# Audio tower with mixture of experts: a drain behind each gather and scatter of GpSimd, and another order of a bias' split, slots and one-hots

## The chip, the cores and the metric

The kernel runs on one core of one Trainium2 chip. The metric is the device time of one launch in microseconds, as the median of several executions. The engines are TensorE (PE in the rows), VectorE (DVE), ScalarE (ACT), GpSimd (POOL) and SyncE (SP); each has its own instruction order, and semaphores tie them together.

## What is computed

Sixteen recordings of 64 channels and 750 samples are cut into patches of 200 samples, which gives 4096 tokens. Each passes a Fourier transform and a two-layer network into 128 features, then attention with sparsemax (8 heads, 256 tokens per sequence), then eight experts, each of which chooses its own 1024 tokens. The part that the change is about is the last one:

```python
x_flat = x.reshape(N, Dd)                      # N = 4096, Dd = 128
logits = x_flat @ Wr                           # 8 experts
probs = jax.nn.softmax(logits, axis=0)         # over the tokens
vals, idx = jax.lax.top_k(probs.T, C)          # C = 1024 for each expert
selected = x_flat[idx]
h = gelu(einsum('ecd,edf->ecf', selected, W1) + b1)      # F = 512
out_e = einsum('ecf,efd->ecd', h, W2) + b2
output = zeros_like(x_flat).at[idx.reshape(-1)].add(vals[..., None] * out_e)
```

The kernel computes in f32, with bf16 for masks and one-hots.

## The kernel before

**Up to the routing.** The spectrum and sixteen rounds of attention, one for each 512 tokens, follow a plan (`PLAN`, `STEPS`) that fixes the order of TensorE's, ScalarE's and VectorE's work. GpSimd only does small things there: `power()` (lines 505 to 508), the reciprocal square root of a layer norm, and `anymore()` (line 514). The normalised rows go to the DRAM tensor `rows2`.

**Routing.** VectorE takes the largest logit of each expert, GpSimd reduces it over the partitions (line 558), then ScalarE exponentiates, VectorE sums, and GpSimd reduces again (line 560). Fifteen steps of `two_bits` find each expert's threshold; `ranks` then numbers the chosen tokens. Before line 558 GpSimd splits the output bias of expert 7 into three bf16 parts (lines 538 to 556). The build puts a change of GpSimd's configuration (MODIFY_POOL_CONFIG) ahead of the first reduction, and another behind the second.

**Expert 7** is computed densely for all tokens (`every_hidden`, `every_out`), in between the other work. VectorE adds its rows to `h` with weights (`every_added`, line 1673, 32 instructions for all 4096 tokens); ScalarE tells through the semaphore `every_y_ok` that rows are there.

**Experts 0 to 6** pass a pipeline of six steps:

1. `one_hots(e)` on VectorE (lines 1606 to 1625) builds one-hot matrices from the ranks; line 1603 is one of their 32 comparisons, line 1615 the largest multiplication.
2. `expert_slots(e)` on TensorE (line 1106) multiplies them, and `slots(e)` on VectorE (lines 1631 to 1643) turns the product into 1024 row numbers.
3. `gather(e)` on GpSimd (lines 575 to 582): 8 indirect DMAs of 128 rows of 512 bytes from `rows2` into `xg`.
4. `expert_columns`, `expert_hidden`, `expert_out` on TensorE (lines 1115, 1130, 1144) with ScalarE's copies and gelus (line 631).
5. `weighted(e)` on VectorE (lines 1650 to 1669), in two halves: line 1662 adds the bias in PSUM, line 1664 multiplies by the weights into `y`. The semaphore `y_ok` counts the halves.
6. `scatter(e)` on GpSimd (lines 584 to 606): 8 indirect DMAs of 128 rows into the expert's own plane in DRAM, 4 for each half. Between the halves of experts 1 to 5 one DMA adds the plane of the expert before to `h` (line 600). A wait ahead of the fifth scatter (line 592) lets VectorE reuse `y`.

GpSimd's order is gathers 0 to 3, then scatter 0, gather 4, scatter 1, gather 5, scatter 2, gather 6, scatters 3 to 6. Line 587 is the wait for the first half of `y`, line 578 that for a gather's slots. Its sequencer runs ahead of its cores: requests wait in a queue. TensorE does expert e+1's columns between expert e's first and second layer, and slots for expert e+3 behind these columns. VectorE's order is one-hots, slots, and `weighted` of three experts before.

Behind the last scatter a no-op (line 617) raises `issued`; VectorE then adds plane 5 (line 1708), SyncE loads plane 6 in quarters, VectorE adds them (line 1714) and SyncE stores the result.

Of the kernel before, what the change touches and what calls it, by code (L numbers as in the profile page):

```python
# [130 lines left out]
def audio_tower(nc, x, tok_w1, tok_b1, tok_w2, tok_b2, w_qkv, w_out, b_out, w_r, e_w1, e_b1, e_w2, e_b2,  # L131
# [25 lines left out]
    E = w_r.shape[1]  # L157
# [13 lines left out]
    with ctx:  # L171
# [311 lines left out]
        def _(g):  # L483
# [53 lines left out]
            attention_round(BEFORE)  # L537
            power()
            g.wait_ge(sems["every_w_in"], 64)
# [15 lines left out]
            g.drain()  # L555
            g.engine_nop().then_inc(sems["b2_ok"], 1)
            g.wait_ge(sems["mx_in"], 1)
            g.partition_all_reduce(all_max[:, :], lg_max[:, :], P, RMAX).then_inc(sems["mx_ok"], 1)
# [16 lines left out]
            def gather(e, p, half=range(CT)):  # L575
                g.wait_ge(sems["slots_ok"], e + 1)
                g.wait_ge(sems["xg_used"], e + 1)
                g.sem_inc(sems["pool_held"], 1)
                for s in half:
                    g.indirect_dma_start(xg[p][:, s, :], None, rows2[:, :],  # L580
                                         bass.IndirectOffsetOnAxis(ap=gather_at[p][:, s:s + 1], axis=0))\
                        .then_inc(sems[f"xg_in{p}"], 16)

            def scatter(e):
# [3 lines left out]
                for s in range(CT):  # L588
                    if s == CT // 2:
# [3 lines left out]
                        if 0 < e < GE - 1:  # L593
# [3 lines left out]
                            else:  # L597
# [7 lines left out]
                    g.indirect_dma_start(plane[e][:, :], bass.IndirectOffsetOnAxis(ap=add_at[p][:, s:s + 1], axis=0),  # L605
                                         y[p][:, s, :], None).then_inc(sems[f"y_out{p}"], 16)

            g.sem_inc(sems["y_free"], 2)
# [11 lines left out]
        def _(a):  # L620
# [167 lines left out]
            every_gelu(4, 1, c.job(1))  # L788
            every_out(3)
            every_gelu(5, 0, c.job(3))  # L790
            every_gelu(5, 1, c.job(1))
# [31 lines left out]
        def _(t_):  # L823
# [298 lines left out]

            def expert_hidden(n, p, ahead=None):
                t_.wait_ge(sems[f"ew_in{p}"], (n + 1) * 64)
                jobs = []
                for m in range(F // P):
# [5 lines left out]
                    done(jobs[-1], last)  # L1132
                    if m == 1 and ahead is not None:
                        expert_slots(ahead)
# [22 lines left out]
            columns_used(expert_columns(0, 0))  # L1157
            hidden = expert_hidden(0, 0, 2)
            columns = expert_columns(0, 1)
# [9 lines left out]
            for e in range(1, GE):  # L1169
                hidden = expert_hidden(e // 2, e % 2)  # L1170
                if e + 1 < GE:
                    columns = expert_columns((e + 1) // 2, (e + 1) % 2)
                    if e + 3 < GE:
                        expert_slots(e + 3)
                    columns_used(columns)
                expert_out(e % 2, hidden)

        @block.vector
        def _(v):
# [500 lines left out]
            one_hots(1, quarters=True)  # L1680
            slots(0, 1, first=True)
            one_hots(2)
            slots(1, 0)
            c.up("slot3", 1)
            one_hots(3)
            slots(1, 1)
            v.tensor_tensor(every_w[:, :], pr[:, E - 1, :], sel[:, E - 1, :], ALU.mult)
            v.wait_ge(sems["every_y_ok"], 1)
            v.drain()
            every_added(range(0, 6))  # L1690
            weighted(0, 0)
            v.wait_ge(sems["every_y_ok"], 2)
            v.sem_inc(sems["held"], 1)
            every_added(range(6, 8))
            v.drain().then_inc(sems["every_ok"], 1)
            for e in range(4, GE):
                one_hots(e)
                slots(e // 2, e % 2)
                weighted((e - 3) // 2, (e - 3) % 2)
            for e in range(GE - 3, GE):  # L1700
                weighted(e // 2, e % 2)
# [57 lines left out]
```

## Time and profile before

| | |
|---|---|
| median of 3 runs | 884.61 us (882.42 to 889.73) |
| the profiled execution, as a run | 887.41 us |
| its span, first to last instruction | 885.6 us |
| mean granted TensorE clock | 0.912 of full speed |
| PE busy | 720.7 us (81%) |
| DVE busy | 604.1 us (68%) |
| ACT busy | 473.0 us (53%) |
| POOL busy | 163.7 us (18%), 121 us of it behind 660 us |
| chain that ended last | PE 35%, DVE 32%, issue 13%, ACT 6%, an unknown queue 4% |

The chain of work that ended last is followed back from the last instruction, at each step to what released it; "issue" is time in which the engine waited for nothing that the profile shows, and "remote" or "another core or an unknown queue" is a wait whose releaser it does not find. Busy time leaves out waits, semaphores and the sequencers' work. A name with a q (POOLq) is an engine's sequencer. For a gather or scatter the row's duration is GpSimd's making of descriptors, not the transfer.

### The profile page before, as it was taken

How to read it: one execution, taken by the hardware profiler on the slowest of the kernel's cores; microseconds unless marked ns; L12 is line 12 of the kernel's file. 1: busy time of each engine (PE TensorE's matmuls, PEld its weight loads, DVE VectorE, ACT ScalarE, POOL GpSimd, SP SyncE). 2: the span in 40 equal slices, each digit the busy share in tenths (PEclk: the TensorE clock that was granted, in tenths of full speed). 3: DMA queues.
4: the chain of work that ended last, by engine and by line, in shares of the span. 5: the costliest groups of instructions: out<-in, count | busy, mean ns of one | idle time of the engine just before them, and what ended most of it. 6: DMA issues, size and time to landing. Idle time of an engine off the chain costs nothing.

```text
span 885.6 us, 13171 instructions
## 1 busy us (share of the span) xinstructions
PE 720.7 (81%) x4268; PEld 470.2 (53%) x4268; DVE 604.1 (68%) x2163; ACT 473.0 (53%) x697; POOL 163.7 (18%) x213
## 2 busy tenths in 40 slices
PE   5598769768999999999999987776977966855970
PEld 3244355456575575665755755544654645543750
DVE  1877787788979968979689688717886562440124
ACT  3857647447777777877787778533322320122220
POOL 1000000001001010010000100021006575555451
PEclk9889989979999999999999999777988998877995
DMA  7791000000000000000000000020001121675778
GB/s 249 278 333 48 1 1 1 0 1 14 1 2 14 1 2 13 1 14 1 1 13 2 13 1 14 25 65 1 1 2 43 36 70 42 152 155 118 160 165 291
DMA packets 29608, 51.99 MB, mean 59 GB/s; under 512 B 8299, under 2 KB 22976, under 8 KB 27658
## 3 DMA queue, kind: packets, MB, share of 16 engines
q1 hardware_dynamic: 24358, 33.03, 11.8%
q0 software_dynamic: 4944, 17.83, 8.8%
q8 instruction: 34, 0.56, 0.3%
q14 instruction: 60, 0.49, 0.2%
q10 hardware_dynamic: 212, 0.08, 0.0%
HBM read 40.97 MB, written 22.54 MB: 72 GB/s over the span
## 4 chain that ended last, share of the span: by engine, by line
PE 35%; DVE 32%; issue 13%; ACT 6%; DVEq 4%; another core or an unknown queue 4%; POOL 2%; DMA 2%; POOLq 1%; ACTq 1%; SPq 0%
PE ps L903 5%; DVE back L1285 4%; PE ps L1130 4%; PE ps L1144 4%; DVE top L1288 3%; PE ps L948 3%; DVE top L1256 3%; DVE back L1263 3%; PE ps L921 3%; PE ps L858 2%; PE ps L997 2%; PE ps L971 2%; DVE front L1603 2%; ACT front L631 2%
## 5 line engine op out<-in xcount | busy, mean ns | idle before, releaser
L631 ACT ACTIVATE front<-ps 128x1024 f32<-128x1024 f32 (+1 forms) x136 | 132.4, 1001 | 81.5 <-PE ps L884 45.0
L741 ACT ACTIVATE front<-front,minus_tau 128x256 f32<-128x256 f32 x256 | 108.6, 497 | 39.0 <-DVE minus_tau L1384 37.9
L981 PE MATMUL ps<-ident,front 128*128 128x128 f32 x512 | 75.3, 295 | 31.6 <-ACTq L743 22.7
L981 PEld LDWEIGHTS ps<-ident,front 128*128 128x128 f32 x512 | 63.6, 152 | 54.3 <-ACTq L743 32.8
L631 ACT ACTIVATE back<-ps 128x1024 f32<-128x1024 f32 (+2 forms) x79 | 77.5, 981 | 23.5 <-PE ps L981 12.2
L631 ACT ACTIVATE front<-ps,back 128x1024 f32<-128x1024 f32 x28 | 31.0, 1113 | 105.6 <-remote 59.5
L514 POOL CROSS_LANE_REDUCE more_all<-more 128x1 int32<-128x1 f32 x32 | 11.5, 358 | 399.1 <-DVEq L1309 265.7
L1130 PE MATMUL ps<-back 128*128 128x512 f32 x112 | 60.8, 699 | 27.0 <-ACT front L631 14.8
L580 POOL DMA_INDIRECT back<-rows,back x56 | 59.5, 1062 | 81.7 <-issue 53.8
L997 PE MATMUL ps<-back,front 128*64 128x256 f32 x512 | 69.3, 400 | 1.3 <-ACT back L631 1.2
L1285 DVE MATCH_REPLACE8 back<-top,front 128x256 f32<-128x256 f32 x176 | 69.7, 409 | 0.0
L971 PE MATMUL ps<-front 64*128 64x256 f32 x512 | 66.5, 394 | 2.0 <-issue 1.2
L1662 DVE TENSOR_TENSOR ps<-ps,back 128x512 f32<-128x512 f32 x14 | 9.8, 699 | 84.1 <-PE ps L1144 48.8
L1256 DVE MAX8 top<-front 128x8 f32<-128x256 f32 x168 | 58.7, 413 | 9.2 <-issue 5.9
L605 POOL DMA_INDIRECT plane<-back x56 | 54.4, 972 | 41.8 <-DVEq L1669 20.9
L1288 DVE MAX8 top<-back 128x8 f32<-128x256 f32 x176 | 59.7, 412 | 1.6
L948 PE MATMUL ps<-xcur,wqkv 128*128 128x512 f32 x128 | 57.9, 605 | 2.0 <-ACT front L663 1.3
L1144 PE MATMUL ps<-back,front 128*128 128x128 f32 x448 | 53.3, 281 | 6.2 <-ACT back L631 4.0
L1144 PEld LDWEIGHTS ps<-back,front 128*128 128x128 f32 x448 | 52.3, 197 | 7.7 <-issue 7.7
L971 PEld LDWEIGHTS ps<-front 64*128 64x128 f32 x512 | 47.1, 189 | 16.4 <-issue 10.2
L1130 PEld LDWEIGHTS ps<-back 128*128 128x128 f32 x112 | 24.4, 227 | 57.4 <-issue 39.6
L921 PE MATMUL ps<-w2t,hid 128*128 128x128 f32 x384 | 46.9, 284 | 8.8 <-ACT hid_r L699 7.4
(211 smaller groups left out, 1255.9 us busy)
## 6 DMA issues: line engine op xcount, KB each, us to landing
h<-plane POOLq DMA_DIRECT2D x5, 2048.0 KB
back<-in_L_ffn_W_dram SPq DMA_DIRECT2D x16, 256.0 KB
front<-in_x_dram SPq DMA_DIRECT2D x4, 750.0 KB, 5.7
plane<-hid SPq DMA_DIRECT2D x2, 1024.0 KB, 6.3
rows<-xn SPq DMA_DIRECT2D x8, 256.0 KB, 2.2
front<-plane SPq DMA_DIRECT2D x1, 2048.0 KB, 8.5
front<-plane SPq DMA_DIRECT2D x4, 512.0 KB, 5.4
out_dram<-h SPq DMA_DIRECT2D x4, 512.0 KB, 4.5
```

The lines of the kernel that those rows point to most:

```text
L631: a.activation(dst, ps[s][:, 0:cols], func, **kw).then_inc(sems[f"free{s}"], 1)
L741: a.activation(prob[n % 2][:, r, :], sc[n][:, r, :], ACT.Relu, bias=minus_tau[:, n // 2, n % 2 * 4 + r:n % 2 * 4 + r + 1])
L921: mm(o[:, at:at + D], hid[:, m, j * P:(j + 1) * P], w2t[:, m, :], start=(j % 2 == 0 and m == 0), stop=False)
L948: last = mm(o[:, q * 512:(q + 1) * 512], wqkv[:, m * P:(m + 1) * P], xcur[:, :], start=True, stop=True)
L971: last = mm(o[:, a_ * 512 + it * SEQ:a_ * 512 + (it + 1) * SEQ], z[r, hp, b * SEQ + it * P:b * SEQ + (it + 1) * P], z[r, 4 + hp, b * SEQ:( ...
L981: last = nc.tensor.transpose(o[:, a_ * 512 + jb * SEQ + it * P:a_ * 512 + jb * SEQ + (it + 1) * P], prob[n % 2][:, 2 * a_ + it, jb * P:(jb ...
L997: last = mm(o[a_ * DH:(a_ + 1) * DH, hp * SEQ:(hp + 1) * SEQ], v_sb[p][:, 2 * b + jb, hd * DH:(hd + 1) * DH], prob_t[n % 2][:, 2 * a_ + jb ...
L1130: last = mm(o[:, q * 512:(q + 1) * 512], ew1[p][:, m * P:(m + 1) * P], xg_t[:, q * 512:(q + 1) * 512], start=True, stop=True)
L1144: last = mm(o[:, s * D:(s + 1) * D], eh[:, k, s * P:(s + 1) * P], ew2[p][:, k, :], start=(k == 0), stop=(k == F // P - 1))
L1256: v.max(top[d % 2][:, r, 0:8], sc[2 * d + r // 4][:, r % 4, :])
L1285: v.match_replace(sc2[:, r, :], top[d % 2][:, r, 0:8], sc[2 * d + r // 4][:, r % 4, :], LOWEST)
L1288: last = v.max(top[d % 2][:, r, 8:16], sc2[:, r, :])
```

## The change

GpSimd gets a drain behind each of the 56 gather and 56 scatter requests. The split of the bias stands ahead of the last `power()`. On TensorE the slots of expert e+3 come in the middle of expert e's first layer (behind its second quarter, for expert 0 behind the first) and no longer behind the next expert's columns. On VectorE the additions of expert 7 are in groups of 16, 8 and 8 between slots and one-hots, each behind its own signal of ScalarE, which gets one more of them; `weighted` follows the one-hots of four experts later and stands ahead of their slots. The computation is the same.

```diff
--- before.py
+++ after.py
@@ -535,7 +535,6 @@
             attention_round()
             attention_round(("hid", "emb"))
             attention_round(BEFORE)
-            power()
             g.wait_ge(sems["every_w_in"], 64)
             left = vb2
             for n in range(3):
@@ -554,6 +553,7 @@
             g.memset(vb2_one[:, :], 1.0)
             g.drain()
             g.engine_nop().then_inc(sems["b2_ok"], 1)
+            power()
             g.wait_ge(sems["mx_in"], 1)
             g.partition_all_reduce(all_max[:, :], lg_max[:, :], P, RMAX).then_inc(sems["mx_ok"], 1)
             g.wait_ge(sems["sm_in"], 1)
@@ -580,6 +580,7 @@
                     g.indirect_dma_start(xg[p][:, s, :], None, rows2[:, :],
                                          bass.IndirectOffsetOnAxis(ap=gather_at[p][:, s:s + 1], axis=0))\
                         .then_inc(sems[f"xg_in{p}"], 16)
+                    g.drain()
 
             def scatter(e):
                 p = e % 2
@@ -604,6 +605,7 @@
                         g.sem_inc(sems["pool_held"], 1)
                     g.indirect_dma_start(plane[e][:, :], bass.IndirectOffsetOnAxis(ap=add_at[p][:, s:s + 1], axis=0),
                                          y[p][:, s, :], None).then_inc(sems[f"y_out{p}"], 16)
+                    g.drain()
 
             g.sem_inc(sems["y_free"], 2)
             for e in range(4):
@@ -787,6 +789,7 @@
             every_gelu(4, 0, c.job(3))
             every_gelu(4, 1, c.job(1))
             every_out(3)
+            a.drain().then_inc(sems["every_y_ok"], 1)
             every_gelu(5, 0, c.job(3))
             every_gelu(5, 1, c.job(1))
             every_out(4)
@@ -1120,7 +1123,7 @@
                 emptied(job)
                 t_.sem_inc(sems["xg_used"], 1)
 
-            def expert_hidden(n, p, ahead=None):
+            def expert_hidden(n, p, ahead=None, behind=1):
                 t_.wait_ge(sems[f"ew_in{p}"], (n + 1) * 64)
                 jobs = []
                 for m in range(F // P):
@@ -1130,7 +1133,7 @@
                         last = mm(o[:, q * 512:(q + 1) * 512], ew1[p][:, m * P:(m + 1) * P],
                                   xg_t[:, q * 512:(q + 1) * 512], start=True, stop=True)
                     done(jobs[-1], last)
-                    if m == 1 and ahead is not None:
+                    if m == behind and ahead is not None:
                         expert_slots(ahead)
                 return jobs
 
@@ -1155,7 +1158,7 @@
             every_out(5, 0)
             every_out(5, 1)
             columns_used(expert_columns(0, 0))
-            hidden = expert_hidden(0, 0, 2)
+            hidden = expert_hidden(0, 0, 2, behind=0)
             columns = expert_columns(0, 1)
             every_hidden(7, 0)
             every_hidden(7, 1)
@@ -1167,12 +1170,9 @@
             every_out(7, 0)
             every_out(7, 1)
             for e in range(1, GE):
-                hidden = expert_hidden(e // 2, e % 2)
+                hidden = expert_hidden(e // 2, e % 2, e + 3 if e + 3 < GE else None)
                 if e + 1 < GE:
-                    columns = expert_columns((e + 1) // 2, (e + 1) % 2)
-                    if e + 3 < GE:
-                        expert_slots(e + 3)
-                    columns_used(columns)
+                    columns_used(expert_columns((e + 1) // 2, (e + 1) % 2))
                 expert_out(e % 2, hidden)
 
         @block.vector
@@ -1679,25 +1679,28 @@
             c.up("slot3", 1)
             one_hots(1, quarters=True)
             slots(0, 1, first=True)
+            v.tensor_tensor(every_w[:, :], pr[:, E - 1, :], sel[:, E - 1, :], ALU.mult)
             one_hots(2)
+            v.wait_ge(sems["every_y_ok"], 1)
+            v.sem_inc(sems["held"], 1)
+            every_added(range(0, 4))
             slots(1, 0)
             c.up("slot3", 1)
             one_hots(3)
-            slots(1, 1)
-            v.tensor_tensor(every_w[:, :], pr[:, E - 1, :], sel[:, E - 1, :], ALU.mult)
-            v.wait_ge(sems["every_y_ok"], 1)
-            v.drain()
-            every_added(range(0, 6))
-            weighted(0, 0)
             v.wait_ge(sems["every_y_ok"], 2)
             v.sem_inc(sems["held"], 1)
-            every_added(range(6, 8))
-            v.drain().then_inc(sems["every_ok"], 1)
+            every_added(range(4, 6))
+            slots(1, 1)
             for e in range(4, GE):
                 one_hots(e)
+                weighted((e - 4) // 2, (e - 4) % 2)
                 slots(e // 2, e % 2)
-                weighted((e - 3) // 2, (e - 3) % 2)
-            for e in range(GE - 3, GE):
+                if e == 4:
+                    v.wait_ge(sems["every_y_ok"], 3)
+                    v.sem_inc(sems["held"], 1)
+                    every_added(range(6, 8))
+                    v.drain().then_inc(sems["every_ok"], 1)
+            for e in range(GE - 4, GE):
                 weighted(e // 2, e % 2)
             v.wait_ge(sems["issued"], 1)
             v.sem_inc(sems["held"], 1)
```

## Rows read from the trace of the kernel before

**Rows 1.** Timeline, GpSimd, 600:886: start, us, engine, line, operation; idle before, releaser
```profile
663.42 1.50 POOL L580 DMA_INDIRECT back<-rows,back  x1 [38.88 <-issue]
...
734.72 0.99 POOL L580 DMA_INDIRECT back<-rows,back  x1 [5.63 <-DVEq L1636]
736.01 0.96 POOL L580 DMA_INDIRECT back<-rows,back  x1 [0.30 <-issue]
...
825.73 0.96 POOL L605 DMA_INDIRECT plane<-back  x1 [8.93 <-DVEq L1669]
```

**Rows 2.** The same timeline: GpSimd's last scatter
```profile
867.77 0.96 POOL L605 DMA_INDIRECT plane<-back  x1 [0.31 <-issue]
```

**Rows 3.** Timeline, TensorE, 655:886: first layer of experts 5 and 6
```profile
826.72 7.03 PE L1130 MATMUL ps<-back 128*128 128x512 f32 x16
...
843.44 7.03 PE L1130 MATMUL ps<-back 128*128 128x512 f32 x16
```

**Rows 4.** Timeline, all engines, 736:753 us
```profile
735.76 7.05 PE L1144 MATMUL ps<-back,front 128*128 128x128 f32 x55
...
751.86 0.70 DVE L1662 TENSOR_TENSOR ps<-ps,back 128x512 f32<-128x512 f32 x1 [11.01 <-remote]
```

**Rows 5.** Waits, 700:870: engine, line, waited for; us, times, longest
```profile
DVE ps L1662 <- remote: 33.0, 3, 12.1
```

**Rows 6.** Single lines L587 and L592, short windows: durations ns, first and last start
```profile
L587 POOLq EVENT_SEMAPHORE  x1: 17/17/17, 740.9 to 740.9; - x1
...
L592 POOLq EVENT_SEMAPHORE  x1: 17/17/17, 742.9 to 742.9; - x1
...
L587 POOLq EVENT_SEMAPHORE  x1: 17/17/17, 825.0 to 825.0; - x1
```

**Rows 7.** Timeline, GpSimd, 540:602: two operations with a drain between
```profile
588.11 0.52 POOL L545 TENSOR_TENSOR back<-back 3x128 f32<-3x128 f32 x1 [0.15 <-issue]
588.76 0.36 POOL L542 CAST back<-back 3x128 bf16<-3x128 f32 x1
```

**Rows 8.** Line L171 alone, 860:886: GpSimd's drain at the end
```profile
L171 POOLq DRAIN  x1: 9331/9331/9331, 863.9 to 863.9; - x1
```

**Rows 9.** Single lines L580, L605, L600: durations ns min/median/max, starts
```profile
L580 POOL DMA_INDIRECT back<-rows,back x56: 940/944/4682, 663.4 to 801.3; - x56
...
L605 POOL DMA_INDIRECT plane<-back x56: 954/962/1033, 719.1 to 867.8; - x56
...
L600 POOL DMA_DIRECT2D h<-plane x5: 1337/1363/1391, 749.6 to 847.2; - x5
```

**Rows 10.** Timelines, VectorE and GpSimd: gathers held up by VectorE
```profile
698.60 1.89 POOL L580 DMA_INDIRECT back<-rows,back  x1 [0.30 <-issue]
...
707.88 4.68 POOL L580 DMA_INDIRECT back<-rows,back  x1 [0.30 <-issue]
...
705.35 6.39 DVE L1673 SCALAR_TENSOR_TENSOR h<-front,h 128x128 f32<-128x128 f32 x24
```

**Rows 11.** Timeline, VectorE, 640:886: the addition behind the last scatter
```profile
870.54 4.42 DVE L1708 TENSOR_TENSOR h<-h,front 128x4096 f32<-128x4096 f32 x1 [9.65 <-DMA front<-plane]
```

**Rows 12.** Around the reductions: timelines of GpSimd, VectorE, ScalarE; lines L558, L567
```profile
586.70 1.02 POOL L507 TENSOR_TENSOR rstd<-var_eps,minus_half 128x4 f32<-128x4 f32 x1 [15.68 <-DVE var_eps L1494]
...
592.48 0.42 DVE L1518 TENSOR_REDUCE lg_max<-lg 128x8 f32<-128x256 f32 x1 [3.02 <-ACT lg L711]
...
L558 POOLq MODIFY_POOL_CONFIG  x2: 11/11/11, 593.1 to 593.1; - x2
...
599.22 0.39 POOL L558 PARTITION_ALL_REDUCE all_max<-lg_max  x1 [6.28 <-issue]
...
602.75 0.67 ACT L769 ACTIVATE front<-front 128x256 f32<-128x256 bf16 x1
...
L567 POOLq MODIFY_POOL_CONFIG  x2: 8/8/8, 602.7 to 602.7; - x2
...
609.63 0.84 POOL L567 TENSOR_TENSOR front<-front 128x256 f32<-128x256 f32 x1 [6.90 <-issue]
```

## Prediction

> **What bounds the kernel now.** I read the chain of work that ended last first, then the timelines of GpSimd, VectorE, TensorE and ScalarE in the last quarter of the span, where all but one part of the diff lies. Up to 663 us the kernel is bound by VectorE and TensorE, and GpSimd is nearly idle. From 663.42 us on, GpSimd issues 56 gathers and 56 scatters, and the last scatter's descriptors are out at 868.73 us [rows 1, 2]. After that come 16.9 us of landing, adding and storing, which nothing in the diff changes. So the question is how long that stretch of 205.3 us becomes.
>
> It is not bound by one engine. TensorE can do an expert in 16.7 us: that is the distance between the first-layer matmuls of the last two experts, 826.72 and 843.44 us [rows 3]. GpSimd needs 8 gathers and 8 scatters of 1.25 to 1.27 us each and one plane addition, some 22 us, for an expert that has both. Yet from 740.88 to 751.86 us VectorE waits with no releaser that the profile names: the TensorE matmuls for which it waits had ended at about 742.8 us by their row, and it resumes only at 751.86 [rows 4]. VectorE's waits of this kind before line 1662 sum to 33.0 us in three places [rows 5], each while GpSimd issues a gather and the first half of a scatter without pause. The reader is to see two things: these freezes are dear, and they sit beside long unbroken bursts of descriptor work.
>
> **The drains.** 112 are added. Now the requests lie ready in GpSimd's queue, and the gap between one and the next is 0.30 us (second gather of a group, 736.01 us) [rows 1]. With a drain behind each, the sequencer may take up the next request only when the last is done, so its work on a request no longer hides. How long is that? The first scatter of an expert starts at 825.73 us, 0.75 us after the semaphore wait of line 587 at 825.0 us is over [rows 1, 6]; and between the wait of line 587 at 740.9 and the one of line 592 at 742.9 lie just four scatters, 0.49 us each, while GpSimd was still busy with older ones [rows 6]. Both say that the sequencer spends about half a microsecond on a request, and about 0.3 us pass before the first descriptor. The drain itself: between small operations on GpSimd with a drain between them the gap is 0.13 us (588.63 to 588.76) [rows 7], of which I take 0.05 us as the drain. So the gap grows from 0.30 to 0.80 us, and the period from 1.25 to 1.75 us.
>
> The Trainium skill, page "DMA: Bandwidth & Descriptors", section "Anatomy of one DMA — SWDGE (gpsimd) path", gives some 50 ns for the sequencer's dispatch of such a DMA; the 0.49 us above disagree with it. By the page the gap would be about 0.35 us and GpSimd's sum, an estimate, some 160 us, where rival 2 below arrives from rows.
>
> The bounds. Below: if only the drain's 0.05 us is added to the gap of 0.30 us, the period is 1.30 us. Above: the trace has one drain behind such requests, the last one of GpSimd. It begins at 863.9 us and lasts 9.331 us, to 873.2 us, while the last scatter's descriptors were done at 868.73 [rows 2, 8]. These are 4.5 us that no row explains. If they are a backlog of the last 8 requests, each drain costs another 0.56 us and the period is 2.31 us. If every drain waited 4.5 us, the period would be 6.25 us; I hold that for unlikely, since the no-op in front of that drain released VectorE before 870.54 us.
>
> Now the sum for GpSimd, if it never waits for others. Work: 56 x 0.944 + 56 x 0.962 = 106.7 us [rows 9], and 0.56 us because the first gather takes 1.50 [rows 1]. Gaps: 111 x 0.80 = 88.8 us. Five plane additions, 1.36 us each [rows 9] with a gap of 0.30: 8.3 us. Lockout by VectorE: one gather takes 4.68 us from 707.88 on, while VectorE adds up `h` with two inputs in SBUF [rows 10]; that is 3.7 us over the usual; and two more gathers, one of them at 698.60, take 1.89 us beside line 1615 [rows 10]; I keep 5.6 us in all. Sum 210.0 us, against 205.3 now: **+4.7 us**. A gather's or scatter's data is in time in this sum: TensorE's 16.7 us per expert fit into 16 x 1.75 + 1.7 = 29.7 us, and in the last experts, which have no gather, into 8 x 1.75 + 1.7 = 15.7 us nearly. What is late next when the freezes go is thus GpSimd itself, and the 33 us of [rows 5] turn into its gaps.
>
> Behind the last scatter stands a drain too, ahead of the no-op that releases VectorE's last additions. If it costs as little as the others, nothing; if it ends at 873.2 us as in [rows 8], the addition of 4.42 us now at 870.54 [rows 11] ends at 877.7 instead of 874.96, 2.7 us later. I take **+1 us**.
>
> **The bias' split.** It moves ahead of `power()`, into 15.68 us in which GpSimd waits for line 1494, so `power()` is no later [rows 12]. The reduction over partitions (line 558) behind it: now the change of configuration stands at 593.1 and the reduction at 599.22, with its input ready at 592.90 [rows 12]. Those 6.1 us are on the chain. Does that cost begin at the configuration change, which moves to the end of `power()` at 587.7 us, or at the reduction's dispatch? The second such change answers: it stands at 602.7, ScalarE's result that line 567 waits for comes at 603.4 (602.75 + 0.67), the operation runs at 609.63 [rows 12]. From the change that is 6.9 us, from the wait's end 6.2, and 6.1 at the first place. So the cost follows the wait, and the move gains only **-0.2 us**. Counted from the change it would gain 593.1 - 587.7 = 5.4 us; I keep that for the range.
>
> The Trainium skill, page "GPSIMD Engine Reference", section "Instruction dispatch", gives about 6 us for this code load, measured as the gap "minus the event-wait"; by that rule, as by my reading, an earlier configuration change gains next to nothing.
>
> **The order of slots, one-hots and additions.** No instruction is added but one ScalarE drain and three waits with their increments; the sixteen or eight additions stand where VectorE waited. Slots for expert e+3 come during expert e's first layer, one-hots ahead of `weighted`. This lets gather 4 start right behind scatter 0 instead of 5.6 us later (GpSimd's idle time before 734.72) [rows 1]. While GpSimd is the bound, that gain is already in the sum, which lets it never idle; VectorE's and TensorE's own work is hidden by GpSimd's 29.7 us per expert. If the bound were elsewhere, it would be worth up to those 5.6 us.
>
> Total: 4.7 + 1 - 0.2 = +5.5 us. The profiled execution spans 885.6 us and took 887.41 as a run; the median of the runs shown is 884.61. Against that median the forecast is **890 us**.
>
> **Rivals.**
> 1. *The freezes stay.* If they come from GpSimd's requests as such and not from their density, the waits of [rows 5] remain, and each burst on the path is longer by its drains: 8 scatters before the idle time at 729.1, three bursts of 12 requests, the last 8: 52 x 0.5 = 26 us, so 884.6 + 26 = **911 us**. For it: nothing in the trace shows that a gap of 0.8 us is enough. Against: behind a burst VectorE is released about a microsecond after GpSimd falls quiet [rows 4], and in the last experts, with pauses, no wait without a name appears.
> 2. *The drains are nearly free* (the side opposite to my number): the period is 1.30 us. GpSimd's sum is 106.7 + 0.6 + 111 x 0.35 + 8.3 + 5.6 = 160 us, 45 less than now: **840 us**. For it: the lower bound above; and that four requests passed in 2.0 us may hide waiting. It decides at a period of 1.62 us, where the sum falls by 1%. Against: the 0.75 us between wait and first scatter recur at each group.
> 3. *A drain waits for more than its request*, 0.56 us each: 111 x 0.56 = 62 us on top, **952 us**. For it: [rows 8]. Against: it is a single drain at the block's end.
>
> **How the numbers follow.** Forecast (period 1.66 to 1.9): 0.4, its own range 880 to 908. Rival 1: 0.15. Rival 2, with all periods below 1.66: 0.3, spread from 840 to 876. Rival 3 and beyond: 0.15. What a measurement here can tell from no change is about 1%, 8.8 us. Faster by more than that: rival 2, 0.3. Slower: rivals 1 and 3 and a quarter of the forecast's share, 0.4. The same: the rest, 0.3. The range of 8 in 10 leaves out the fast end of rival 2 and the slow end of rival 3: 850 to 930 us.
>
> **What would show it.** In the timeline of GpSimd: the distance between the starts of two gathers, 1.75 us if I am right, 1.3 under rival 2, 2.3 under rival 3; GpSimd without idle time from gather 2 to the last scatter. In the waits: no wait without a name before line 1662 if the freezes are gone, some 33 us if rival 1 holds. Around 599 us: the reduction at 599.0, or at 593.9 if the code load starts at the configuration change. Most likely to be wrong is the period, since each 0.1 us of it moves the result by 11 us.

## The result, and the profile after

The forecast of 890 us was wrong, and so was its range. Median of the changed kernel 1100.13 us (1098.48 to 1104.99), of the kernel before beside it 884.73 us: ratio 1.242, interval 1.236 to 1.248. The change costs 215 us.

The profiled execution took 1100.87 us, its span is 1099.1 us. The mean granted TensorE clock fell from 0.912 to 0.829, and TensorE now waits through most of the last part, where the page's tenths of the clock are 5 to 8 (5 is the lower of its two levels, 1.2 GHz, all through a slice). Sections 2 and 4 of the page:

```profile
PE   4787796899999999999877984596405233073000
POOL 1000000101010000000011003232332222322221
PEclk9799797999999999999877997698757657576555
...
issue 32%; PE 23%; DVE 22%; POOLq 13%; ACT 4%; DVEq 3%; POOL 2%; ACTq 1%; DMA 1%; SPq 0%
POOLq L583 6%; POOLq L608 6%; PE ps L906 4%; DVE back L1285 4%; DVE top L1288 3%; PE ps L951 2%; DVE top L1256 2%; PE ps L1000 2%; PE ps L984 2%; PE ps L924 2%; PE ps L861 2%; DVE back L1263 2%; PE ps L974 2%; PE ps L871 2%; PE ps L1011 1%
```

Two drain lines, 583 behind the gathers and 608 behind the scatters, hold 12% of the chain; nothing of the kind was there before. The first gather starts at 655.66 us, against 663.42 in [rows 1]; most of these 7.8 us need not come from the change, since the kernel before, traced again in run 8, starts it at 656.69. The timeline of GpSimd, first gathers (start, duration; idle before):

```profile
655.66 1.50 POOL L580 DMA_INDIRECT back<-rows,back  x1 [38.80 <-DVEq L1636]
659.51 0.95 POOL L580 DMA_INDIRECT back<-rows,back  x1 [2.35 <-issue]
662.90 0.94 POOL L580 DMA_INDIRECT back<-rows,back  x1 [2.43 <-issue]
666.18 0.94 POOL L580 DMA_INDIRECT back<-rows,back  x1 [2.34 <-issue]
```

The gap is 2.3 to 2.4 us where it was 0.30 [rows 1] and where I had forecast 0.80. The same view around a plane addition (line 601) of an expert in the middle:

```profile
886.70 0.97 POOL L606 DMA_INDIRECT plane<-back  x1 [2.07 <-issue]
889.72 0.96 POOL L606 DMA_INDIRECT plane<-back  x1 [2.05 <-issue]
892.71 0.96 POOL L606 DMA_INDIRECT plane<-back  x1 [2.04 <-issue]
895.72 1.32 POOL L601 DMA_DIRECT2D h<-plane  x1 [2.05 <-issue]
897.34 1.03 POOL L606 DMA_INDIRECT plane<-back  x1 [0.30 <-issue]
912.07 0.96 POOL L606 DMA_INDIRECT plane<-back  x1 [13.70 <-issue]
```

Scatters come every 3.0 us. The addition has no drain behind itself, so the fifth scatter follows at 0.30 us; but the drain behind that scatter holds GpSimd for 13.7 us. The two drains as single lines (durations in ns, minimum, median, maximum), and the median times in us from issue to landing, which is when all of a request's sixteen semaphore increments have come:

```profile
L583 POOLq DRAIN  x56: 2484/2820/4075, 655.4 to 944.1; - x56
...
L608 POOLq DRAIN  x56: 2515/2529/15107, 767.6 to 1082.0; - x56
...
h<-plane POOLq DMA_DIRECT2D x5, 2048.0 KB, 14.5
...
back<-rows,back POOLq DMA_INDIRECT x56, 2.5
...
plane<-back POOLq DMA_INDIRECT x56, 2.2
```

A drain lasts about as long as its request takes to land. Single landings in the trace say it closer: 107 of the 112 drains end 0.07 to 0.08 us after the request in front of them has landed, and the five behind an addition 0.12 to 0.13 us after. The longest, 15.1 us, is about as long as the 2 MB of the addition take, 14.5 us; the scatter behind that addition (897.34) itself needs 13.9 us to land, where others need 2.2. Waits behind 655 us (engine, line, waited for; us, times, longest):

```profile
DVE back L1650 <- POOLq L593: 241.4, 5, 60.7
POOL plane L606 <- issue: 166.9, 56, 13.7
ACT front L633 <- PE ps L1133: 166.7, 28, 55.4
POOL back L580 <- issue: 130.3, 54, 3.6
```

Everybody waits for GpSimd now: VectorE 241 us at line 1650 for the release of `y` (`y_free`, line 593), which GpSimd raises only when it gets past its own drains. GpSimd itself waits for hardly anybody: behind the first gather its idle time is "issue", but for one gap of 2.51 us before a gather. The waits without a name of [rows 5] are gone.

### The profile page after: what moved, and what is told of

Same layout as the page of the kernel before. It is cut to its first block, busy times and chain, and to the rows that moved or that the text cites. A ratio compares the mean times of both kernels' runs of the same rounds, so it can differ in the third digit from the quotient of the medians.

```text
span 1099.1 us, 13285 instructions
## 1 busy us (share of the span) xinstructions
PE 730.1 (66%) x4268; PEld 479.5 (44%) x4268; DVE 603.2 (55%) x2163; ACT 473.6 (43%) x697; POOL 160.5 (15%) x213
## 4 chain that ended last, share of the span: by engine, by line
issue 32%; PE 23%; DVE 22%; POOLq 13%; ACT 4%; DVEq 3%; POOL 2%; ACTq 1%; DMA 1%; SPq 0%
POOLq L583 6%; POOLq L608 6%; PE ps L906 4%; DVE back L1285 4%; DVE top L1288 3%; PE ps L951 2%; DVE top L1256 2%; PE ps L1000 2%; PE ps L984 2%; PE ps L924 2%; PE ps L861 2%; DVE back L1263 2%; PE ps L974 2%; PE ps L871 2%; PE ps L1011 1%
## 5 line engine op out<-in xcount | busy, mean ns | idle before, releaser
L1147 PE MATMUL ps<-back,front 128*128 128x128 f32 x448 | 60.4, 304 | 46.2 <-DVE back L1664 41.6
L580 POOL DMA_INDIRECT back<-rows,back x56 | 55.8, 996 | 171.6 <-issue 130.3
L1147 PEld LDWEIGHTS ps<-back,front 128*128 128x128 f32 x448 | 59.4, 219 | 48.5 <-issue 48.5
L606 POOL DMA_INDIRECT plane<-back x56 | 55.1, 984 | 166.9 <-issue 166.9
L1118 PE MATMUL ps<-ident,back 128*128 128x128 f32 x56 | 11.9, 382 | 84.0 <-DMA back<-rows,back 84.0
L1133 PE MATMUL ps<-back 128*128 128x512 f32 x112 | 58.0, 671 | 8.6 <-DMA back<-in_L_ffn_b_dram 7.3
L974 PEld LDWEIGHTS ps<-front 64*128 64x128 f32 x512 | 47.4, 190 | 16.5 <-issue 10.2
L906 PE MATMUL ps<-back,w1m 101*128 101x512 f32 x96 | 51.8, 622 | 2.3 <-issue 2.3
## 6 DMA issues: line engine op xcount, KB each, us to landing
h<-plane POOLq DMA_DIRECT2D x5, 2048.0 KB, 14.5
```

The costliest lines, as they stand in the source:

```text
L906: last = mm(o[:, m % 2 * 512:(m % 2 + 1) * 512], w[:, m * P:(m + 1) * P], f[:, ds(g * 512, 512)], start=(w is w1m), stop=(w is w1a))
L974: last = mm(o[:, a_ * 512 + it * SEQ:a_ * 512 + (it + 1) * SEQ], z[r, hp, b * SEQ + it * P:b * SEQ + (it + 1) * P], z[r, 4 + hp, b * SEQ:( ...
L1147: last = mm(o[:, s * D:(s + 1) * D], eh[:, k, s * P:(s + 1) * P], ew2[p][:, k, :], start=(k == 0), stop=(k == F // P - 1))
```

## The experiments

The kernels ran in four groups, each on one chip. The kernel before took 883.52 us in the first group and 886.39 in the third (the first chip), 852.22 in the second (a second chip) and 852.47 in the fourth (a third). These 31 to 34 us are themselves a finding, below; until then, times are only compared within a group.

The theory: a drain on GpSimd waits until the software DMAs issued before it have landed. The rivals: a drain has a fixed price of about 2 us that has nothing to do with the transfer; or the new order of slots, one-hots and additions made the time, by a circle of waits.

**1. Order without drains.** The changed kernel, the two added drains taken out:

```diff
                         .then_inc(sems[f"xg_in{p}"], 16)
-                    g.drain()
...
                                          y[p][:, s, :], None).then_inc(sems[f"y_out{p}"], 16)
-                    g.drain()
```

> The changed kernel without its 112 drains: the split ahead of power(), slots, one-hots and additions in the new order, gathers and scatters issued back to back as before. Theory 1 (the whole loss is the drains, since a drain ends only when the request's data has landed): GpSimd's period falls back from 3.0-3.3 to 1.25 us and the time to below the kernel before: 884.7 less 5.4 for the reduction at line 558 and up to 5.6 for the idle time ahead of gather 4, so 874 to 880 us; VectorE's waits without a named releaser ahead of line 1662 stay near 33 us, since the requests are as dense as before. Rival (part of the loss is the new order, for instance scatter 0 held up by its wait for every_ok, or weighted behind one-hots): above 890 us.

Measured: 873.63 us (870.77 to 877.91), ratio 0.986 (0.982 to 0.990) to the 883.52. Split and order gain 9.9 us by the medians, 12.5 by the ratio; they aren't what costs.

**2. Drains alone**, in the kernel before:

```diff
                         .then_inc(sems[f"xg_in{p}"], 16)
+                    g.drain()
...
                                          y[p][:, s, :], None).then_inc(sems[f"y_out{p}"], 16)
+                    g.drain()
```

> The kernel before with a drain behind each gather and scatter and nothing else. Theory 1: the chain of GpSimd is the same as in the changed kernel, so 1100 us plus the 5.4 us of the reduction, 1100 to 1115 us, and no wait without a named releaser is left on VectorE. Rival (drains and new order do harm together): 1000 us or less.

Measured: 1111.14 us in a single run, so the drains cost 227.6 us, and split and order still gain some 11 us beside them.

**3. The split alone**, `power()` behind it:

```diff
             attention_round(BEFORE)
-            power()
             g.wait_ge(sems["every_w_in"], 64)
...
             g.engine_nop().then_inc(sems["b2_ok"], 1)
+            power()
```

> The kernel before with power() moved behind the split of the bias and nothing else. If the code load ahead of the reduction of line 558 starts at the change of configuration, as the changed kernel's 591.5 us against 599.2 suggests: the reduction comes some 5.4 us earlier relative to its input and the kernel takes 879 us. If it starts when the reduction's input is ready, as I predicted: 884.5 us, no change.

Measured: 879.11 us (875.88 to 884.11), ratio 0.995 (0.992 to 0.998): 4.4 us faster. Its change of configuration and its reduction (single line 558), and the timeline there:

```profile
L558 POOLq MODIFY_POOL_CONFIG  x2: 11/11/11, 584.9 to 584.9; - x2
...
589.28 0.42 DVE L1518 TENSOR_REDUCE lg_max<-lg 128x8 f32<-128x256 f32 x1 [2.72 <-ACT lg L711]
590.55 0.39 POOL L558 PARTITION_ALL_REDUCE all_max<-lg_max  x1 [5.62 <-DVE lg_max L1518]
```

The input is there at 589.70 and the reduction runs 0.85 us later; from the change of configuration to it are 5.6 us. In [rows 12] it was 593.1 to 599.22, 6.1 us, with the input there before. So the wait runs inside the 5.6 us, not ahead of them. The same distance is 5.7 us in the changed kernel and 5.9 in run 10's order without drains (581.9 to 587.76), each with the input there 0.9 to 1.0 us before the reduction.

**4. Waiting for the landing instead of draining.** The changed kernel, with each drain replaced by a wait for the request's own sixteen increments (the scatters alike):

```diff
-                    g.drain()
+                    g.wait_ge(sems[f"xg_in{p}"], (e // 2) * (16 * CT) + 16 * (s + 1))
+                    g.sem_inc(sems["pool_held"], 1)
```

> The changed kernel with each of the 112 drains replaced by a wait for the request's own 16 semaphore increments. Theory 1 (a drain of GpSimd waits for the landing of the outstanding requests): the same period, 3.0 to 3.3 us, and 1095 to 1105 us. Rival (the drain has a cost of its own, for instance by slowing the transfer or the restart of the sequencer): the requests land sooner than 1.2 us after their descriptors, the period falls by 0.5 us or more, 1040 us or less.

Measured: 1099.38 us, within 0.1% of the changed kernel. Its chain from the first gather (start, us, what):

```profile
652.46 3.09 DMA back<-rows,back
655.59 0.78 issue
656.37 2.48 DMA back<-rows,back
658.89 0.76 issue
659.65 2.54 DMA back<-rows,back
662.23 0.75 issue
```

Here the chain names what it waits for: 2.5 us from the start of the descriptors to the landing, then 0.75 us until the next request begins. That makes 3.25 us, the period that the drains have. A GpSimd drain behind each gather is thus worth what a wait for its landing is worth. The same holds behind an addition, where the wait is for the increments of the scatter alone (the addition was issued at 829.11):

```profile
830.77 1.04 POOL L607 DMA_INDIRECT plane<-back  x1 [0.30 <-issue]
844.81 0.96 POOL L607 DMA_INDIRECT plane<-back  x1 [12.99 <-DMA plane<-back]
```

The changed kernel has 13.04 us at this place. So the scatter behind 2 MB itself lands late, and a wait for it alone is as long as a drain.

This run and the changed kernel end with the same drain of the block, that of [rows 8]. First run 4, then the changed kernel:

```profile
L171 POOLq DRAIN  x1: 4356/4356/4356, 1083.2 to 1083.2; - x1
```

```profile
L171 POOLq DRAIN  x1: 101/101/101, 1084.6 to 1084.6; - x1
```

In both every request has landed before it. Where a drain stands just before it, it takes 0.10 us; where none has stood behind any of the 117 requests (112 and the five additions), it takes 4.36 us, and 4.35 in run 5. So a drain has a second price, which has nothing to do with landing and grows with the requests since the last drain. In run 9's traces it ends 0.4 to 0.5 us behind the last landing after 9 or 10 requests, and 1.4 us after 33. As an estimate from these numbers that is some 0.04 us for each request.

**5. A stop without the landing**, which is what I had taken the drain for. The order without drains, and behind each request a small fill of a dead tile and a wait for it:

```diff
+                    g.memset(hid_r[:, :], 0.0).then_inc(sems["paced"], 1)
+                    g.wait_ge(sems["paced"], c.up("paced"))
+                    g.sem_inc(sems["pool_held"], 1)
```

> The kernel of e1_order_only with, behind each gather and scatter, a small fill of a dead tile on GpSimd and a wait of its sequencer for that fill: a drain that ends when the descriptors are made and does not wait for the data. This is the drain that the prediction assumed. Theory 1 (the sequencer's 0.7 us and a pause between requests are all there is to a drain but the landing): a period of 1.8 to 2.0 us, GpSimd never idle, 112 x 1.9 + 14 = 227 us from the first gather at 658, so 895 to 910 us; and if the freezes come from requests that follow each other within 0.3 us, VectorE has no wait without a named releaser. Rival (the freezes come from the requests as such): those waits stay near 40 us and the time goes above 915 us.

Measured: 925.05 us, beside 852.22 of the kernel before on that chip. Timeline of GpSimd:

```profile
661.28 0.34 POOL L583 MEMSET hid_r<- 128x256 f32 x1
662.43 0.97 POOL L580 DMA_INDIRECT back<-rows,back  x1 [0.81 <-POOL hid_r L583]
663.40 0.38 POOL L583 MEMSET hid_r<- 128x256 f32 x1
664.58 0.96 POOL L580 DMA_INDIRECT back<-rows,back  x1 [0.81 <-POOL hid_r L583]
```

The gap behind the fill is 0.81 us: the 0.80 that I had worked out for the sequencer's restart. The fill's own 0.33 us makes the period 2.1 us. Of the forecast's period the restart was right and the drain itself was not. My figure for this run, 895 to 910, was too low, and wrongly made from the first chip's time besides. Of the freezes this run tells nothing, as its whole group has none.

**6. No requests for experts 4 to 6.** Order without drains, where these gathers are replaced by fills and a small operation, so that the rows of three experts are wrong; descriptor work and transfers of 24 gathers are missing.

> The kernel of e1_order_only in which gathers 4 to 6 are left out: in place of each of their 24 requests GpSimd fills a slice of the tile (0.2 us) and raises four elements to a power (1.0 us), so that it is busy as long, but makes no descriptors and nothing is transferred; experts 4 to 6 work on constants. Theory 1 (long unbroken runs of descriptor making freeze the other engines): with runs of 4 scatters and one plane addition only, the waits without a named releaser behind 730 us, about 33 us in e1_order_only, fall below 5 us, and the kernel takes 835 to 850 us. Rival (GpSimd's being busy, or the full queue of its instructions, freezes them): the waits stay, 870 to 878 us.

Measured: 836.28 us, in the range, but by luck: it was to show whether freezes vanish with the requests, and no trace of this group has freezes, those with all requests neither. It tells nothing of them.

**7. Fewer drains**: behind every fourth request (21, those behind a scatter's second half left out) and behind every eighth gather (7). Both in the order without drains; the lines of the first, in `gather` (in `scatter` the condition is `s == 3`; the second kernel has `s == CT - 1` in `gather` alone):

```diff
+                    if s % 4 == 3:
+                        g.drain()
```

> The kernel of e1_order_only with a drain only behind the fourth and eighth request of a gather and the fourth of a scatter: 21 drains at about 2.0 us each (1.3 us landing, 0.7 us restart) in place of a gap of 0.3. Theory 1 (unbroken runs of some 7 requests cause the freezes, and a pause ends them): GpSimd's work is 142 + 14 + 42 = 198 us and it is nearly never idle, waits without a named releaser below 10 us, 865 to 875 us. Rival (pauses do not help): the freezes stay and 12 to 20 us of drains come on top, 885 to 895 us.

> The kernel of e1_order_only with one drain behind the last request of each gather, 7 in all, about 2.0 us each. Theory 1: the runs are cut to 8 gathers and 4 scatters with a plane addition; a freeze can begin within the 8 gathers only near their end and is over at the drain, so the waits without a named releaser fall from 41 us to 15 or less and the time to 855 to 868 us. Rival (pauses do not help): 874 to 885 us.

Measured: 896.27 us, ratio 1.053 (1.048 to 1.058), and 860.62 us, ratio 1.013 (1.007 to 1.018), to 852.22. The first is a miss: I had supposed that 21 pauses find cover. Two of its drains, the first behind a scatter with an addition, leave gaps of 8.27 and 6.82 us. The second lies in its range of 855 to 868 by luck, since that was made from the first chip's 874 less its freezes.

**8. The same on the first chip again**, with the kernel before itself, to see whether the second group had lost its freezes by its kernels or by its chip:

> The kernel before itself, once more. Theory A: the freezes (waits without a name, 33.0 us in three places at line 1662) belong to the kernel, and the batch whose kernel before took 852 us lacked them because of the changes in those four kernels; then they are in this trace whatever its time. Theory B: they belong to the chip or to the run; then a trace of some 852 us has none, and one of some 883 us has 30 us of them.

> The changed kernel without its 112 drains, once more. If split and order are worth the same on every chip: 9 to 10 us below the kernel before (ratio 0.989). If half of the gain was that the order dodges freezes, then on a chip without freezes only the split's 5 us are left (ratio 0.994).

> One drain behind each eighth gather, 7 in all, once more beside the same kernel with none. A drain that waits for landing costs some 2 us and GpSimd has 2 to 3 us to spare per expert: 0 to 10 us above the kernel with no drains. Theory B adds: on a chip with freezes the seven pauses could win up to 10 us; on one without they win nothing.

Measured, beside 886.39 us: before itself 882.87; order without drains 876.40 (ratio 0.989, 0.985 to 0.993); one drain per eight gathers **867.00** (ratio 0.979, 0.975 to 0.983), the fastest on this chip. The waits behind 655 us, of the kernel before, then of the order without drains, then of that with seven drains:

```profile
DVE ps L1662 <- remote: 35.1, 3, 12.2
```

```profile
DVE ps L1660 <- remote: 41.2, 5, 12.2
```

```profile
DVE ps L1662 <- remote: 20.5, 5, 7.4
```

Freezes are in each. At this line seven pauses halve them; over all lines the "remote" waits fall from 113.9 to 88.6 us, by a fifth. The very kernel that loses 1.3% on the second chip gains 2.1% on this one.

**9. Only the gathers' drains, only the scatters', and no plane additions.** The first ran in the third group, the others in the fourth.

> The changed kernel with the drains behind the 56 gathers alone. If a drain waits for its request to land, gathers start every 3.3 us and scatters every 1.27: four gathers up front to 760 us, three experts of some 36 us each, three of 17, and 17 us at the end: 940 to 965 us. If the drains' cost were a fixed price on any request, half of the 225 us between this kernel without drains and the changed one: 980 to 990 us.

> Drains behind the 56 scatters alone. GpSimd if never idle: 56 x 1.25 + 51 x 3.0 + 5 x 16.4 = 305 us from 656 us on, and 17 us at the end: 978 us, or a little more with waits: 978 to 1005. If gathers' and scatters' costs simply added up (1100 - 99): 1001 us. If drains behind scatters were cheap: under 940 us.

> The changed kernel with all its drains, but without the five plane additions on GpSimd (a no-op raises their semaphore; the planes' sums are missing from the output). If the drain behind the fifth scatter waits for the addition's landing as well (13.7 us instead of 2.05), the time falls by 5 x (1.35 + 0.3 + 11.7) = 67 us, to 1033 us. If that long drain only overlapped other waiting, it falls by the additions' own 5 x 1.65 = 8 us, to 1092 us.

Measured: 975.32 us (third group, order without drains 876.40: +98.9); 992.59 us (fourth group, order without drains 844.68: +147.9); and without the additions, with all 112 drains, 1046.45 us. That is some 54 us less than the changed kernel, though that one was timed on a chip where the kernel before takes 885. Neither trace has a freeze, and the stretch of GpSimd alone, from the first gather to the end of the last scatter's descriptors, says the same: 372.2 us (656.56 to 1028.80) against 427.5. Of the 67 expected for a drain that waits behind the addition, most is there (the 67 took the longest gap, 13.7 us, for all five; their mean is 12.9), and the 8 us of the rival are excluded. The scatters' run, 992.59, is in its range of 978 to 1005. The gathers' run was over its range by 10 us. Its timeline of GpSimd shows why, at the first gather after a scatter with an addition:

```profile
811.40 1.39 POOL L602 DMA_DIRECT2D h<-plane  x1
...
829.79 0.96 POOL L580 DMA_INDIRECT back<-rows,back  x1 [10.57 <-issue]
833.20 0.94 POOL L580 DMA_INDIRECT back<-rows,back  x1 [2.45 <-issue]
```

Nothing waited for the addition behind the scatters, which have no drains here; the second gather of the group still waits 10.57 us where its neighbours wait 2.4. The gather in front of that drain, issued at 818.23, is itself late:

```profile
L580 POOL DMA_INDIRECT back<-rows,back x1: 997/997/997, 818.2 to 818.2; - x1
...
DMA to landing us min/median/max: 10.4/10.4/10.4
```

It lands at 828.6, 1.1 us behind the addition (811.40 + 16.1 = 827.5), and the drain ends 0.5 us later, at 829.0. So a drain pays for an addition that is still on its way. Whether it waits for the addition itself, or only for the small request that lands behind it, no run here tells apart: in each the last request is also the last to land, and in run 4 the wait for that request alone is as long.

**10. Before itself and the order without drains on the third chip.**

> The kernel before itself again. Freezes belong to the kernel: 33 us of nameless waits at line 1662 in any case. Freezes belong to the chip: none where it takes some 852 us, 30 to 35 us where it takes some 885.

> The changed kernel without drains again. On a chip as in the first batch: 9 to 10 us below the kernel before. On the one where the kernel before takes 852 us: 5 us below if only the split is worth something there, 10 if the order is too; above 852 if the order costs where no freezes are, as the 860.6 us of the same kernel with 7 drains suggest.

Measured, beside 852.47 us: 853.75, and **844.68** (839.98 to 848.35, ratio 0.991, 0.987 to 0.994), the fastest time of all runs whose computation is whole. The waits of the kernel before here, behind 655 us:

```profile
DVE ps L1662 <- PE ps L1144: 38.1, 12, 8.4
...
DVE back L1650 <- POOLq L592: 20.9, 3, 9.3
```

No wait is "remote". The same program has 33.0 us of them at line 1662 [rows 5] and, again, 35.1 us in run 8. What a freeze looks like on TensorE shows best in the order without drains, second layer of an expert, first on the first chip, then on the third:

```profile
705.94 0.37 PE L1145 MATMUL ps<-back,front 128*128 128x128 f32 x1 [0.33 <-issue]
706.64 0.51 PE L1145 MATMUL ps<-back,front 128*128 128x128 f32 x3 [0.33 <-issue]
707.41 0.48 PE L1145 MATMUL ps<-back,front 128*128 128x128 f32 x2 [0.27 <-issue]
```

```profile
709.61 6.60 PE L1145 MATMUL ps<-back,front 128*128 128x128 f32 x57 [1.60 <-ACT back L631]
```

On one chip 57 matmuls run in one piece; on the other, one to three at a time, with "issue" between, while GpSimd makes descriptors. That TensorE lacks instructions or operands there is a guess; no run told it. The difference between the chips lies wholly in the stretch that has the freezes: from the first gather to the end of the last scatter's descriptors the kernel before takes 207.7 us in run 8 (656.69 to 864.38) and 173.5 here (660.82 to 834.28). Nor are dense scatters alone enough for a freeze: run 9's kernel with drains behind the gathers only, on the first chip, has no "remote" wait.

## Why the prediction was wrong

**The step that failed: the drain itself.** I took 0.05 us for it, from two small operations on GpSimd with a drain between them [rows 7]. Those leave nothing outstanding but the cores' own work. A gather's descriptors are made in 0.95 us, but its data land 2.5 us after the start, and run 4 shows the drain worth a wait for that landing. So the gap is 2.5 - 0.95 = 1.55 us of landing plus 0.75 of restart: 2.3 us, against 0.05 + 0.75. The restart, from [rows 6], was right: 0.75 to 0.78 us in run 4, 0.81 in run 5.

**The row that had it.** [rows 8] stood in the prediction: the only drain of the old trace that has software DMAs in front of it ended 4.5 us after the last descriptors. I wrote "4.5 us that no row explains", divided it by 8 to make a rival, and set aside the reading that each drain waits. The old chain of waits has the last scatter's landing at 871.09 us, 2.4 us behind its descriptors; that is the part which the change multiplies by 112. For the other 2.1 us runs 4 and 5 have a likely source: a drain that none precedes takes 4.4 us behind 117 requests, even with all of them landed (run 4). In the changed kernel, where every gather and scatter has its own drain, this price is at most 0.13 us for each, and 4.5 us for every drain would have been wrong too. My reason, that the no-op in front released VectorE early, is no reason: a no-op isn't a drain. In the changed kernel the no-op stands behind a drain. The Trainium skill, page "DMA: Bandwidth & Descriptors", section "Anatomy of one DMA — SWDGE (gpsimd) path", fits a software DMA by 2.0 us and its bytes at 436e3 per us; for 64 KB that gives an estimate of 2.15 us. This case's trace agrees nearly, with 2.2 us for a scatter and 2.5 for a gather. I had used this section for its 50 ns of dispatch, which the trace contradicts (0.49 us, [rows 6]), and not for the landing.

**The sum with the right term.** In the changed kernel, from the first gather on, by the page's groups and the waits: 55.8 + 55.1 us of making descriptors, 5 x 1.33 for the additions; idle before gathers 171.6 - 38.8 (ahead of the first) = 132.8, before scatters 166.9, before the additions 5 x 2.05 = 10.2. That is 427.5 us, and 655.66 + 427.5 = 1083.2 is where the last scatter's descriptors end (1082.21 + 0.96). So "GpSimd never idle" but for its own drains was the right frame, with 210.0 us in it where 427.5 belong. Of the missing 217.5 us the five drains behind additions take 54, a term that the sum lacked altogether: their gaps, 12.1 to 13.7 us with a mean of 12.9, are 10.9 us over the ordinary 2.05. The rest is the period, 3.0 us for scatters and 3.3 for gathers in place of 1.75. One more long gap, 6.24 us before the scatter at 1063.99, stands beside SyncE's load of 2 MB issued at 1055.93; run 4 has 6.27 there, put down to the landing. And 890 + 217.5, less 5.2 for the split (below) and 1 for the last drain, is 1101.3 us.

**The last drain**, +1 us in my sum: VectorE's addition (line 1711, start 1084.95) comes 1.8 us behind the last scatter's descriptors, as it did before (870.54 - 868.73 in [rows 2, 11]), but for another reason: before it was held by the load of plane 5, `DMA front<-plane` in [rows 11], now by the no-op behind the drain (1084.6). From the end of the descriptors to the end of the span it is 15.9 us, against 16.9: the last scatter lands 1.3 us behind its descriptors and not 2.4, so SyncE loads plane 6 earlier. The drain added nothing to the time.

**The split**: I took -0.2 us and kept -5.4 for the range. The second was right, 4.4 us by the medians of run 3: the load runs from the change of configuration, and the input's wait lies inside it. In the changed kernel it is at 585.9, the reduction at 591.57. The second change of configuration, from which I had argued [rows 12], had 6.9 us from the change, 6.2 from the wait's end; these couldn't tell the two apart, since the wait there ended only 0.7 us after the change. The Trainium skill, page "GPSIMD Engine Reference", section "Instruction dispatch", gives the load as about 6 us, the gap minus the event-wait. In run 3 the gap is 5.6 us with the wait inside it, so that only 0.85 us are left behind the wait; the measurement disagrees with this rule.

**The order**, worth nothing in my sum: 9.9 us for all but the drains less 4.4 for the split leaves some 5 us by the medians and 8 by the ratios (runs 1 and 3), with some 5 us of uncertainty either way. I had named 5.6 for the case that the bound is elsewhere [rows 1]; that these are the same 5 us is not shown.

**Freezes**: that they vanish when the requests come less densely was right for the gaps of 2.0 to 2.4 us that came (none in the changed kernel), and rival 1 fell. Whether the forecast's gap of 0.80 would have been enough is open, since run 5, which has it, ran on a chip without freezes. And their 33 us were swallowed by GpSimd's sum, as the prediction said they would be; and seven drains take off only a fifth. The other rivals were on either side of a period of 1.75 us and all below the 3.0 to 3.3 that it became.

## What to carry to other kernels

A drain on the engine that issues software DMAs is here a wait for the landing of the last of them, which comes behind the large ones issued before it: price it by the time from issue to landing plus the restart, here 1.55 + 0.75 us on top of 0.95, and some 11 us more where 2 MB are on their way. A drain that is the first in a long while pays some 0.04 us besides for each request since the last one. Look for what is outstanding in front of a drain before taking its price from a row elsewhere, and when one row doesn't fit the price (the 9.3 us drain here), settle it before dividing it away. What a wait costs can be had on the chip that the trace is from; a gain of a few per cent should be seen on a second chip before it is believed.

## What the hardware showed beyond this

- **Chips differ in freezes.** The kernel before takes 883.52 and 886.39 us (medians) on one chip, and 852.22 and 852.47 on two others. The traces differ by nameless waits of ScalarE and VectorE while GpSimd issues requests at 1.25 us each (ScalarE 60.4 us in all at line 631 in run 8's trace of the kernel before, VectorE 35.1 at line 1662), which the others lack wholly, and by TensorE's matmuls in ones to threes. The prediction's picture of what binds the kernel holds on the first chip only. What in the chip makes them is open.
- **The price of a drain depends on what binds.** Seven drains cost 16 us where nothing freezes (860.62 on the second chip against 844.68 on the third, with the kernel before within 0.3 us on both), 2.3 us each, GpSimd being the bound: behind its first gather it is idle for 50.6 us in the kernel without drains and 66.1 in the one with seven. On the first chip they gain 9.4 us (867.00 against 876.40).
- **A change of configuration loads at once**, 5.6 to 5.9 us, while the instruction behind it still waits (run 3, the changed kernel, run 10). Put ahead of a wait, all but about 0.9 us of it is hidden.
- **A drain's second price.** 0.10 us right behind another drain, 4.36 us behind 117 requests without one, all landed (run 4). What the drain does in that time is open.
